# A division moved from GpSimd to the end of VectorE's step in an attention and feed-forward kernel

## The reference

```
x = x + layernorm(attention(layernorm(x)))
x = x + layernorm(layernorm(x) @ ternary(weight).T * alpha + bias)

attention: qkv = x @ W_qkv + b_qkv; 16 heads of 8, 4 key/value heads
  scores = q . k / sqrt(8), causal; attn = softmax(scores)
  y = attn @ v;  out = y @ W_out + b_out
```

## Time and profile before

| what | us |
|---|---|
| median of 3 runs | 492.5 |
| the runs | 489.48, 492.5, 495.44 |
| the profiled execution | 494.3 |
| its span, first to last instruction | 492.5 |
| TensorE (PE) busy | 419.3 |
| VectorE (DVE) busy | 389.9 |
| ScalarE (ACT) busy | 323.5 |
| GpSimd (POOL) busy | 294.7 |

### The profile page before, as it was taken

One profiled execution on the slowest core, in us unless ns is written; L12 is line 12 of the kernel. 1 busy time (PEld: TensorE's weight loads), 2 busy tenths in 40 slices (PEclk: granted clock), 3 DMA queues, 4 the chain that ended last, 5 costly groups with the idle time before them and its releaser, 6 DMA issues.

```text
span 492.5 us, 18291 instructions
## 1 busy us (share of the span) xinstructions
PE 419.3 (85%) x6918; PEld 291.4 (59%) x6918; DVE 389.9 (79%) x1299; ACT 323.5 (66%) x577; POOL 294.7 (60%) x551
## 2 busy tenths in 40 slices
PE   0321899989999999999999999998999999999641
PEld 0211666666667676767677757775677677665330
DVE  1310878889999999999899989997999998995532
ACT  0220147667778787888888878886788788768521
POOL 0140223356777777777777767775777776756663
PEclk9999999999999999999999999998999999999855
DMA  5757334333632363335333533354333433331121
GB/s 145 170 113 91 52 56 97 77 76 76 116 77 73 79 159 75 75 75 150 76 77 75 148 82 76 77 134 87 68 75 71 120 78 76 75 89 29 28 63 43
DMA packets 77587, 42.85 MB, mean 87 GB/s; under 512 B 13084, under 2 KB 73276, under 8 KB 77500
## 3 DMA queue, kind: packets, MB, share of 16 engines
q1 hardware_dynamic: 77500, 41.68, 38.4%
HBM read 13.85 MB, written 4.72 MB: 38 GB/s over the span
## 4 chain that ended last, share of the span: by engine, by line
PE 57%; DVE 9%; DMA 8%; POOL 7%; issue 7%; SPq 7%; ACT 3%; POOLq 0%; DVEq 0%; ACTq 0%
PE ps_y L802 13%; PE ps_mx L828 12%; PE ps_st L781 11%; PE ps_w L854 6%; DMA den<-Y 4%; DVE M L632 4%; PE ps_w L882 4%; PE ps_w L891 3%; POOL yn L425 3%; PE ps_w L892 2%; SPq L279 2%; PE ps_w L874 2%; DVE stats L590 2%; PE ps_w L841 2%; PE ps_w L864 2%
## 5 line engine op out<-in xcount | busy, mean ns | idle before, releaser
L632 DVE TENSOR_REDUCE M<-ps_mx 128x2 f32<-128x512 f32 (+3 forms) x448 | 219.3, 530 | 42.0 <-PE ps_mx L828 40.2
L457 ACT ACTIVATE PT<-ps_st 128x1024 f32<-128x1024 f32 (+1 forms) x192 | 168.6, 881 | 25.7 <-PE ps_st L781 15.2
L828 PE MATMUL ps_mx<-KS,QS 112*64 112x64 bf16 (+2 forms) x2560 | 133.8, 229 | 23.1 <-DMA KS<-part 19.3
L828 PEld LDWEIGHTS ps_mx<-KS,QS 112*64 112x64 bf16 x2560 | 90.9, 114 | 69.1 <-issue 27.4
L781 PE MATMUL ps_st<-QS,KS 114*64 114x256 bf16 (+1 forms) x1024 | 104.9, 306 | 0.0
L802 PE MATMUL ps_y<-PT,VB 128*32 128x256 f32 (+3 forms) x2048 | 103.8, 309 | 0.9 <-ACT PT L457 0.9
L397 POOL TENSOR_TENSOR rstd<-vareps,mhalf 128x2 f32<-128x2 f32 x128 | 88.9, 694 | 10.0
L432 POOL TENSOR_TENSOR rest<-QK,part 128x512 f32<-128x512 f32 x32 | 37.1, 1160 | 43.2 <-ACT part L486 43.2
L395 POOL TENSOR_TENSOR vareps<-mv,eps 128x2 f32<-128x2 f32 x128 | 25.7, 201 | 54.7 <-DVE mv L602 54.5
L500 ACT CAST MpT<-ps_w 16x512 bf16<-16x512 f32 x32 | 18.4, 575 | 56.3 <-PE ps_w L864 56.3
L781 PEld LDWEIGHTS ps_st<-QS,KS 114*64 114x64 bf16 x1024 | 47.7, 110 | 13.0 <-issue 2.2
(11 more groups left out here) (59 smaller groups left out, 507.6 us busy)
## 6 DMA issues: line engine op xcount, KB each, us to landing
QS<-part SPq DMA_DIRECT2D x192, 64.0 KB
rden<-rec_dram SPq DMA_DIRECT2D x32, 256.0 KB
X<-in_x SPq DMA_DIRECT2D x8, 512.0 KB, 6.3
out<-X SPq DMA_DIRECT2D x8, 512.0 KB, 5.0
KS<-part SPq DMA_DIRECT2D x32, 96.0 KB
QS<-qfb SPq DMA_DIRECT2D x4, 512.0 KB
KS<-part SPq DMA_DIRECT2D x32, 64.0 KB
KS<-kfb SPq DMA_DIRECT2D x4, 264.0 KB
```

Source lines behind the costliest of these rows:

```text
L457: nc.scalar.activation(PT[n % 2][:, 0:512 * banks], ps_st[n % 2][:, 0:banks, :].rearrange("p a c -> p (a c)"), ACT.Exp, scale=SCALE).then_ ...
L632: last = nc.vector.tensor_reduce(m[:, pair:pair + pairs, i], ps_mx[n % 2][:, at:at + w].rearrange("p (h t) -> p h t", h=pairs), AX_X, ALU.max)
L828: last = pe.matmul(ps_mx[n % 2][64 * one:64 * one + 64, at:at + w], q[:, h, BL * i:BL * i + BL], k[:, kv, blocks, :], start=True, stop=Tru ...
```

## The change

The multiplication yn = Y * rden leaves GpSimd's step, where it stood between `remainder` and the second `add_normed`, and is now the last piece of VectorE's step, behind `maxima(s, 9)`. It is the same single instruction on 128 x 512 fp32 elements, it waits for the same two semaphores (rden landed, and the output projection of two batches ago done) and raises the same one. Buffers, transfers and the other engines' lists are unchanged.

```diff
--- before.py
+++ after.py
@@ GpSimd @@
-            def divide(s):
-                if s.on(DIV):
-                    i = s.b(DIV) % 2
-
-                    second(gp, s, DIV, s_shift[i])
-                    free(gp, s, DIV, s_op_ps, bufs=2)
-                    gp.tensor_tensor(yn[i][:], Y[i][:], rden[i][:], ALU.mult).then_inc(s_yn, 1)
-
@@ GpSimd, step @@
                 add_normed(s, OUT, A2, s_a2, s_x1)
                 remainder(s)
-                divide(s)
                 add_normed(s, FFN, F2, s_f2, s_fin)
@@ VectorE @@
+            def divide(s):
+                if s.on(DIV):
+                    i = s.b(DIV) % 2
+
+                    second(dve, s, DIV, s_shift[i])
+                    free(dve, s, DIV, s_op_ps, bufs=2)
+                    nc.vector.tensor_tensor(yn[i][:], Y[i][:], rden[i][:], ALU.mult).then_inc(s_yn, 1)
@@ VectorE, step @@
                 maxima(s, 8)
                 maxima(s, 9)
+                divide(s)
```

## The result

The changed kernel takes 498.67 us (median of 9 runs, 496.25 to 500.53) against 492.5 (median of 9, 489.48 to 496.7) in the same session: ratio 1.011, interval 1.0072 to 1.0148. It is slower, by 1.1%; by this ratio that is 5.4 us, by the medians 6.2. The forecast had the sign and the mechanism, but was too high: 504 us, range 499 to 512, with +11.0 us where the medians differ by 6.2. The two spans (496.7 and 492.5) therefore differ by only 4.2 us, and it is these 4.2 us that the traces can explain.

What follows compares the result with a forecast made beforehand. TensorE, busy all of a 12.33 us step, was taken as the bound, with 0.07 us of slack at bank 2; 16.8 - 0.8 + 0.7 - 1.8 - 2.4 - 1.5 = +11.0 us on 492.5 gave 503.5, forecast 504 us, range 499 to 512.

Steps and rivals of the forecast that it cites:

- the low end: Lower bound of the forecast: 0.46 us a step, +7.5 us in all, less 1.7 for the clock, 498.3 us.
- 0.60 us a step: TensorE's added wait at bank 2 behind the divide and bank 0's reduction: 28 x 0.60 = +16.8 us.
- the relief that I had put at zero: Undisturbed steps: the cast, freed by GpSimd's shorter step, only lengthens VectorE's wait for bank 8; zero.
- 0.07 us of slack: Step's end: TensorE could run bank 2 at 218.89 and took it up at 218.96, VectorE's only room.
- the prediction had named 0.47: TensorE's added wait per step if VectorE's instructions overlap by 0.09 us on both sides of the divide.
- The rival of a full blocking: Divide does nothing while GpSimd's X + F runs; the step costs 0.85 us, 511 us in all; chance 0.09.
- I had put this wait at nothing: Divide's wait of 0.1 us for X + F mostly hides in its start-up; nothing added, 0.19 us for the upper end.
- +1.8 us for the six: Six late-GpSimd steps: the added delay, less the lateness that goes without yn on GpSimd, 6 x -0.25 = -1.5 us.
- The added 0.60 is absorbed there: Four steps where TensorE later waits for VectorE, itself held by den: the delay comes out of those waits, -2.4 us.
- the prediction priced at -1.7: The one drop of the granted clock to 0.50 vanishes: -1.7 us, counted only in the low end.
- Here 1.27 us becomes 0.69: 3 x -0.6: Last three divides, no reduction left and TensorE waiting for yn: shorter on VectorE, -1.8 us.
- the +0.7 of the prediction: The 29th divide stands behind the last bank 9, whereas GpSimd had begun it at 443.01: +0.7 us.

Runs made afterwards that it cites:

- e5: Changed kernel with op ahead of bank 2 on TensorE and VB ahead of bank 0's reduction on VectorE; 493.54 us, ratio 0.9977 to the kernel before.
- e4: Changed kernel with the divide made twice on VectorE, the first into an unused tensor; 515.17 us, ratio 1.0485 to the kernel before.
- e3: Kernel before with GpSimd's divide cut to 2 of 512 columns, the rest of yn zero; 485.22 us, ratio 0.9876 to the kernel before.
- e2: Changed kernel with VectorE's divide cut to 2 of 512 columns, the rest of yn zero; 488.49 us, ratio 0.9858 to the kernel before.
- e9: Changed kernel with GpSimd's X + F moved to the next step, behind part and the first inverse; 498.7 us, ratio 1.0108 to the kernel before.
- e8: Changed kernel with the last three divides back on GpSimd; 500.67 us, ratio 1.0149 to the kernel before.
- e1: Changed kernel with only op put ahead of bank 2 on TensorE; 502.45 us, ratio 1.0231 to the kernel before.
- e7: Changed kernel with VectorE's divide moved to the next step, behind bank 0's reduction and VB; 492.91 us, ratio 1.0006 to the kernel before.
- e11: e5 together with the earlier load of x of e10; 490.65 us, ratio 0.9955 to the kernel before.
- e12: e11 with X + F moved as in e9; 487.7 us, ratio 0.9894 to the kernel before.
- e6: Kernel before, divide on GpSimd, with both reorderings of e5; 494.2 us, ratio 1.003 to the kernel before.
- e10: Kernel before with the load of x issued two steps earlier; 491.7 us, ratio 0.9967 to the kernel before.

## Why the forecast was right in kind and too high

The measured 498.67 us lies 0.3 below the stated range of 499 to 512. The prediction's own working of the low end gave 498.3; the range was then written from 499, above what had been worked out. That is a slip at the edge. The terms are what matters, and the first that was mis-sized is the **0.60 us a step**: it measured 0.47, because the relief that I had put at zero is worth 0.08 and the chain to bank 2 grew by 0.05 less than I took. The late steps of GpSimd were mis-sized the same way, their relief being taken too small; the drain erred the other way. Here is the sum of the prediction beside the two traces, by stretches between bank 8's matmuls. "Before" and "after" are us; the last row holds the bank 8 of the very last batch.

| stretch | before | after | measured | my sum |
|---|---|---|---|---|
| up to the first bank 8 of a full step | 79.25 | 77.66 | -1.6 | 0 |
| 4 intervals of filling | 48.57 | 47.95 | -0.6 | +1.5 |
| 13 undisturbed intervals | 12.33 each | 12.80 or 12.81 | +6.2 | +7.8 |
| 6 intervals with a late GpSimd (12.54 to 12.87) | 76.15 | 76.82 | +0.7 | +1.8 |
| 4 intervals with a late den | 55.69 | 53.52 | -2.2 | 0 |
| the last interval | 11.07 | 11.54 | +0.5 | +0.4 |
| behind the last bank 8 of the full steps | 61.45 | 62.65 | +1.2 | -0.5 |
| sum | | | +4.2 | +11.0 |

**Right, and shown.** The place, the two operations that meet there and 0.07 us of slack: e5 takes bank 0's reduction off that path and the cost goes; e4 doubles the divide and it doubles. The forecast's signs came out: 29 waits for M where 28 were named (though 11.6 us in all and not 15 to 18), yn's waits in full steps gone, VectorE's wait for bank 8 at 0.40, the cast near 0.2, the weight load 0.05 us behind the reduction. The divide alone takes 0.68 to 0.69 us, as taken from the rows.

**The step's size: 0.47 instead of 0.60.** Two parts of it were off. First, VectorE's instructions overlap on both sides of the divide: bank 9's reduction ends at 217.67 and the divide starts at 217.59; the divide ends at 218.42 and the reduction starts at 218.34. For this the prediction had named 0.47. But the divide itself lasts 0.83, since it waits for X + F, so the chain grew by 0.62, where 0.60 + 0.07 = 0.67 stood behind my figure. Less the slack this is 0.55. That it came so close is luck: two errors, an overlap taken too small and a wait for GpSimd taken as nothing, nearly cancel. Second, the part that failed: **"The same relief in the other steps (the cast) comes where TensorE has no wait ...: zero."** It is worth 0.08 us a step, and what it shortens is a wait of TensorE that I had taken not to exist. The kernel before, an undisturbed step; VectorE, then TensorE's weight load for the turn, then its matmuls of bank 2 and of the turn:

```profile
207.61 0.74 DVE L704 CAST Mp<-M 128x32 bf16<-128x32 f32 x1
...
208.65 0.40 DVE L687 TENSOR_TENSOR A<-ps_w,bo_sb 128x256 f32<-128x256 f32 x1
```

```profile
209.16 0.23 PEld L864 LDWEIGHTS ps_w<-idb,Mp 128*16 128x16 bf16 x4 [0.38 <-issue]
```

```profile
206.63 0.40 PE L828 MATMUL ps_mx<-KS,QS 112*64 112x64 bf16 x12
...
209.19 0.38 PE L864 MATMUL ps_w<-idb,Mp 128*16 128x128 bf16 x4
```

The turn writes ps_w, which VectorE's A must first have read. A stood behind the cast, and the cast behind GpSimd's part: in the undisturbed steps the cast ends 0.04 us after part does. The turn's weight load came 0.11 us after A's end (209.05). In the 25 steps that follow the first filling the load comes 0.11 to 0.12 us after A's end each time, while the distance from bank 2 to the turn goes from 2.53 to 3.10; that shows A as what it waits for. The profile calls the load's 0.38 us of idle time "issue", and its matmuls still overlap the ones ahead, so no wait for VectorE is listed. After the change A ends at 221.05 and the load starts at 221.34, right behind the one ahead of it; from bank 2 to the turn it is 221.55 - 219.07 = 2.48 us instead of 2.56. Before, such idle time is put to "issue" 20 times, 7.2 us; after it, once, 0.2 us. The relief doesn't come from taking the divide off GpSimd: in e3, where GpSimd's divide lasts 0.20 us, the cast of the step shown still takes 0.74 us and the turn stands at 2.56. It comes from VectorE being late: its cast now starts at 220.13, when GpSimd's part (ended 220.20) is almost over, instead of early in it. e2 shows the same exchange in small: bank 2 comes 0.03 us later there (2.74 us behind bank 8), the turn 0.03 closer behind it (2.53), and the step stays at 12.33. So the cost is 0.55 - 0.08 = 0.47, and a part of the delay pays for itself.

**X + F and the divide.** GpSimd's X + F ran from 217.14 to 217.87 and the divide ended at 218.42, 0.55 us behind it, not 0.69. The rival of a full blocking would have given 217.87 + 0.69 = 218.56. The rule of the Trainium skill ("SBUF — State Buffer", section "Who interferes with whom"), that a VectorE instruction with two SBUF inputs and a reading GpSimd instruction exclude each other and the later one fully blocks, holds here in that the divide waits, and not for its full length: it ended as if about 0.14 us of it had been done while it waited. In the prediction I had put this wait at nothing, since an overlap of 0.1 us would hide; the divide started 0.09 us earlier in the chain than assumed and X + F ended 0.06 us later, so they meet for 0.28 us, and about 0.15 of it show. e9 measures the same 0.15 from the other side, in the duration and in the step.

**The steps with a late yn or a late GpSimd.** My sum had +1.8 us for the six and +1.5 for the filling; measured, all six are now near 12.80 like the others, and filling is shorter: 1.1 + 2.1 us of the miss. Of the 1.1, 0.8 is again the step's 0.13 (0.60 against 0.47), and of the 2.1, 0.4. In the six steps before, the distance from bank 2 to the turn was 2.77 to 3.10 instead of 2.56, and that is all of their lateness: GpSimd's part, late behind yn, held up VectorE's cast or subtraction, these A, and A the turn. For the rest of the miss I took the landing of rden in those steps as fixed. I think it isn't: a late yn makes part late, that VectorE's subtraction and reciprocal, and with them the next rden. With the divide's length gone from GpSimd the row of late steps ends. e3 supports it (five more steps at 12.33), but these links were not broken one by one.

**The steps with a late den.** The added 0.60 is absorbed there, as said. Beyond it the clock did not fall: the stretch at 0.50 of the earlier trace rows has no counterpart, which the prediction priced at -1.7 and left to the low end. Measured, the four are 2.2 us shorter. The lowered clock shows in the full steps of three of the 14 profiled executions, one of each kernel, so this is more likely luck of the profiled one than a gain; no run separates the two.

**The drain.** Predicted -0.5 us in all, measured +1.2: the failed step is **"Here 1.27 us becomes 0.69: 3 x -0.6"**. TensorE's third op of the drain before, then its second and third in the changed kernel:

```profile
462.96 1.16 PE L854 MATMUL ps_w<-wo_sb,yn 128*128 128x128 f32 x8 [1.47 <-POOL yn L425]
```

```profile
456.98 1.16 PE L854 MATMUL ps_w<-wo_sb,yn 128*128 128x128 f32 x8
...
466.90 2.07 PE L854 MATMUL ps_w<-wo_sb,yn 128*128 128x128 f32 x8 [2.51 <-DVE yn L695]
```

And VectorE between these two:

```profile
459.98 0.35 DVE L713 RECIPROCAL rec<-den 128x32 f32<-128x32 f32 x1 [1.38 <-DMA den<-Y]
...
466.15 0.69 DVE L695 TENSOR_TENSOR yn<-Y,rden 128x512 f32<-128x512 f32 x1 [3.36 <-DMA rden<-rec_dram]
```

From the very last bank 8 to the first op it is 2.66 us instead of 1.93: the +0.7 of the prediction. From the first op to the second it is 8.75 instead of 9.33: one of the three -0.6. From the second to the third it is 9.92 instead of 8.87, 1.05 more, and no gain: the reciprocal waited 1.38 us for den, 2.86 us after den's transfer was issued, where 1.98 had been enough before. From the third to the fourth it is 9.11 instead of 8.87: the divide is shorter, but the clock had gone to 0.50 at 466.32, before this op and not behind it (464.78 before), so that the op took 2.07 us and not 1.16. From there to the end nothing changed (20.68 and 20.66).

How much of this belongs to the change is open. I had counted the shorter operation, and neither the transfers that it waits for nor the clock. VectorE now stands waiting for rden (3.36 us above) with other batches' work behind it, and that may have its part; e8, which was to show it, gave 0.8 us in the drain but no lower total. In the six other kernels with all whole divides on VectorE and made once (e1, e5, e7, e9, e11, e12) this stretch lasted 60.28 to 62.40 us, in e6 and e10, with the divide on GpSimd, 62.38 and 61.29. So the +1.2 can't be told from scatter; that the predicted -1.8 doesn't show is all that holds.

**The head** was 1.6 us shorter with no edit in it. The granted clock rose to 1.00 at 70.37 us instead of 72.25. The head lay between 76.1 and 80.9 us among the kernels run here, so it is scatter.

The misses, -1.6 (head), -2.1, -1.6, -1.1, -2.2, +0.1 and +1.7 (drain), sum to -6.8, from +11.0 to +4.2. About 3.0 us of it is the step's size, 0.13 in each of 23 steps. About half is head and clock, which belong to an execution and not to the change; by medians the change costs 6.2 us, and the 2 us between are not assigned.

## What to carry to other kernels

Before moving work to an engine with idle time, find the next result on that engine for which the bounding engine waits, and measure its slack; an idle share elsewhere in the step is no cover. Then look at what else that waiting instruction depends on before reordering it (e1 lost 0.15 us a step to a second condition, e5 gained 0.43 by moving both). A short operation that no longer stands behind another engine's, or that comes out of a late queue, can be worth more than its busy time in the disturbed steps, so price those steps by letting their lateness go, not by holding the arrivals fixed.

## What the runs showed of the hardware

- On VectorE, a reduction and a divide overlap by about 0.08 us at their boundary, in either order, while two reductions stood 0.03 us apart (218.12 and 218.15, before); a divide of 512 elements lasts 0.68 to 0.69 us and adds 0.61 us to the chain (e4). The Trainium skill ("VectorE: DVE Perf Modes", section on the TRN2 errata) has both a table, from which 512 elements would take (58 + 512) cycles at 0.96 GHz or 594 ns, an estimate, and a fit that gives 691 ns; the duration measured where GpSimd isn't in the way, 677 to 693 ns, is the fit's within 2%.
- A VectorE divide that meets a running GpSimd addition ends less than its own length behind it: 0.55 us where its length alone is 0.69. With small operations it ends almost together with it: the subtraction of the earlier trace rows, 0.19 us by itself, ended 0.04 us after GpSimd's part, and the divide of 2 columns (e2), 0.16 us by itself, 0.02 us after X + F.
- A wait for a buffer can stand under "issue" on the weight load: in the kernel before, the turn's load came 0.11 to 0.12 us after VectorE's A in 25 steps running, and no wait for VectorE is listed. It cost 0.08 us a step.
- GpSimd needs 1.28 us for the product for which VectorE needs 0.69, and 0.20 us for one of 2 columns (e3).
- The granted clock fell to 0.50 within the full steps in three of the 14 profiled executions (before, e3: once for 3.4 us; e2: for 6.8 and 3.4 us) and stayed at 1.00 there in the others. Nine runs of the kernel before spread from 489.48 to 496.7 us, so that a step's saving of 0.15 us (e9, 28 x 0.15 = 4.2 us) can fail to show in the median of four.
